# GNN layer on one core: gathered rows get 32 slots in three of four passes, with a ramp at each pass's start

## The reference, cut to what matters

```python
h = relu(layernorm(x))
h = _gcn_conv(h, src, dst, ones, W1, b1, n)          # pass 0: sum of h[src] per dst, 256 wide after W1
h = h / max(norm(h), 1e-12)
ev  = sigmoid(h[src] @ We1[:H] + h[dst] @ We1[H:])    # a gate for each edge
na  = relu(segment_sum(ev[:, None] * h[src], dst) @ Wn1 + bn1)     # pass 1
ev2 = sigmoid(na[src] @ We2[:H] + na[dst] @ We2[H:])
g   = relu(segment_sum(ev2[:, None] * na[src], dst) @ Wn1 + bn1)   # pass 2
out = _gcn_conv(g, src, dst, ev2, W2, b2, n)          # pass 3, weighted with ev2
return x + out
```

## Time and profile before

| what | value |
|---|---|
| time, median of 3 runs | 3329.52 us (3324.85 to 3332.83) |
| the profiled execution | 3348.71 us, its span 3346.9 us |
| granted TensorE clock, mean | 0.924 |
| busy shares | PE 79%, DVE 63%, ACT 48%, POOL 56% |
| gathers of pass 0 | 129.8 to 899.4 us |
| gathers of pass 1 | 1068.1 to 1701.8 us |
| gathers of pass 2 | 1841.2 to 2535.6 us |
| gathers of pass 3 | 2657.1 to 3288.3 us |
| dense steps of passes 1, 2, 3 end at | 1740.9, 2600, 3322.0 us |

### The profile page before, as it was taken

One profiled execution on the slowest core, in us unless ns is written; L12 is line 12 of the kernel. 1 busy time (PEld: TensorE's weight loads), 2 busy tenths in 40 slices (PEclk: granted clock), 3 DMA queues, 4 the chain that ended last, 5 costly groups with the idle time before them and its releaser, 6 DMA issues.

```text
span 3346.9 us, 58780 instructions
## 1 busy us (share of the span) xinstructions
PE 2635.7 (79%) x16470; PEld 2291.0 (68%) x16470; DVE 2111.6 (63%) x6199; ACT 1617.9 (48%) x3249; POOL 1866.2 (56%) x1816
## 2 busy tenths in 40 slices
PE   0667667898997677777789899999999676777775
PEld 0344446888885667666678788888888566666665
DVE  5567676665635566666675567666676456666667
ACT  7256565666666454554454444444444422233232
POOL 5345456555405666667720666666661267776673
PEclk9788898999999898988899899999999888888998
DMA  4244445555542333333322444444442433333333
GB/s 114 80 147 152 147 155 192 193 208 211 189 174 78 100 100 106 107 98 114 99 71 79 124 134 135 135 135 135 134 134 81 141 98 97 107 106 100 112 99 94
DMA packets 185594, 419.58 MB, mean 125 GB/s; under 512 B 36655, under 2 KB 136700, under 8 KB 175533
## 3 DMA queue, kind: packets, MB, share of 16 engines
q10 hardware_dynamic: 83703, 244.23, 20.6%
q0 software_dynamic: 61472, 140.49, 15.3%
q1 hardware_dynamic: 40118, 31.23, 3.0%
HBM read 311.35 MB, written 102.16 MB: 124 GB/s over the span
## 4 chain that ended last, share of the span: by engine, by line
PE 67%; issue 13%; DVE 9%; ACT 3%; ACTq 3%; another core or an unknown queue 2%; DMA 1%; DVEq 1%; POOL 1%; SPq 0%; POOLq 0%
PE ps L1117 18%; PE ps_high L1109 16%; PE ps_high L1117 12%; PE ps L1057 7%; PE ps_high L1075 3%; PE ps L1041 3%; ACT tab_area L769 2%; PE ps_high L1070 2%; ACTq L377 1%; PE ps_high L1196 1%; DVE acc L1592 1%; DVE tab_area L1521 1%; PE ps L1229 1%; DVE weights L1568 1%
## 5 line engine op out<-in xcount | busy, mean ns | idle before, releaser
L601 POOL DMA_INDIRECT rows<-table,edge_src x1664 | 1759.9, 1058 | 1164.0 <-SPq L496 604.0
L1109 PE MATMUL ps_high<-rows,weights 128*128 x2784 | 648.0, 342 | 385.2 <-issue 235.6
L1117 PE MATMUL ps<-tab_area,acc 128*128 128x129 f32 (+2 forms) x4410 | 824.2, 327 | 7.4 <-issue 6.1
L1109 PEld LDWEIGHTS ps_high<-rows,weights 128*128 128x128 f32 x2784 | 473.6, 204 | 486.9 <-issue 292.9
L1117 PEld LDWEIGHTS ps<-tab_area,acc 128*128 128x128 f32 x4410 | 698.6, 206 | 52.3 <-issue 7.2
L863 ACT ACTIVATE step<-xbuf,rows 128x128 f32 x928 | 358.0, 394 | 690.4 <-PE ps_high L1109 312.8
L1592 DVE TENSOR_TENSOR acc<-acc 128x640 f32<-128x640 f32 x735 | 604.9, 823 | 102.3 <-ACT acc L872 64.7
L1117 PE MATMUL ps_high<-tab_area,acc 128*128 128x129 f32 (+2 forms) x2940 | 588.3, 326 | 0.3 <-issue 0.3
L1575 DVE TENSOR_TENSOR acc<-acc,ps_high 128x129 f32 (+1 forms) x948 | 335.1, 354 | 384.9 <-PE ps_high L1109 187.8
L769 ACT ACTIVATE tab_area<-ps_high x816 | 404.4, 496 | 304.9 <-PE ps_high L1075 178.7
L1117 PEld LDWEIGHTS ps_high<-tab_area,acc 128*128 128x128 f32 x2940 | 478.0, 206 | 29.8 <-issue 1.2
(11 more groups left out here) (242 smaller groups left out, 2177.8 us busy)
## 6 DMA issues: line engine op xcount, KB each, us to landing
acc<-counts ACTq DMA_DIRECT2D x105, 1120.0 KB
counts<-tab_area ACTq DMA_DIRECT2D x51, 1568.0 KB
acc<-counts ACTq DMA_DIRECT2D x25, 1568.0 KB
rows<-table,edge_src POOLq DMA_INDIRECT x1664
table<-tab_area SPq DMA_DIRECT2D x6, 903.0 KB, 4.8
table<-acc SPq DMA_DIRECT2D x7, 448.0 KB, 4.2
table<-tab_area SPq DMA_DIRECT2D x6, 455.0 KB, 3.9
table<-tab_area SPq DMA_DIRECT2D x6, 448.0 KB, 3.0
```

The costliest lines, as they stand in the source:

```text
L601: nc.gpsimd.indirect_dma_start(rows[:, t % UNROLL, 0:row_floats[k]], None, tables[k], bass.IndirectOffsetOnAxis(ap=edge_src[:, t:t + 1], a ...
L1109: nc.tensor.matmul(ps[DENSE_BANKS + m % PAIR_BANKS][:, 0:WIDTH[k]], weights[:, m % W_RING, :], rows[:, bass.ds(known["slots"][m % UNROLL], ...
L1117: ins = nc.tensor.matmul(ps[j][:, 0:WIDTH[k]], gate_blocks[:, n % S_RING, j * PART:(j + 1) * PART], table[:, h, 0:WIDTH[k]], start=(h == 0 ...
```

## The change

The ring of row slots gets 32 slots in passes 0, 1 and 3 (rows of 128 and 130 words) and keeps 16 in pass 2 (rows of 258 words). `rows` becomes 32 x 130 words a partition (before 16 x 258), and each pass sees it with a stride of its own row width. There are 32 `landed` semaphores; `landed_count` works out what a tile's semaphore has counted to, over passes with different rings. To have semaphores for them, a few others are merged into one each (`flags_sent`, `tab_stored`, `pool_scaled`), with larger counts.

A gather's wait no longer stands at the ring's size: gather t may be `ahead` = min(ring, 8 + t // 4) tiles ahead. The first ten gathers of a pass are free (before 16); gather 16 waits for the relay's entry 10 (before 6), gather 24 for entry 16 (before 14); from gather 32 on the wait is the looser one, and from gather 96 on POOL may be 26 tiles ahead of the relay instead of 10. In pass 2 `ahead` ends at 16 with gather 32, which is the wait of before.

As slots differ between passes, DVE computes `pair_row`'s slot numbers anew for 16 slots after pass 1 and for 32 after pass 2 (`row_slots`).

```diff
+FIRST_AHEAD = 8
+SLOT_RING = 32
+ROW_RING = (SLOT_RING, SLOT_RING, UNROLL, SLOT_RING)
...
-        rows = sb("rows", [PART, UNROLL, ROW])
+        rows = sb("rows", [PART, SLOT_RING * ROW1])
...
+        rows_of = [within(rows, 0, [ROW_RING[k], row_floats[k]]) for k in range(4)]
...
-        landed = [sem(f"landed{u}") for u in range(UNROLL)]
+        landed = [sem(f"landed{u}") for u in range(SLOT_RING)]
...
+        def landed_count(k, t):
+
+            slot = t % ROW_RING[k]
+            earlier = sum(HALF // ROW_RING[q] for q in range(k) if slot < ROW_RING[q])
+            return 16 * (earlier + t // ROW_RING[k] + 1)
...
-                        sp.wait_ge(landed[u], tiles_before(k) + 16 * (i + 1))
+                        sp.wait_ge(landed[(i * UNROLL + u) % ROW_RING[k]], landed_count(k, i * UNROLL + u))
                         sp.sem_inc(tiles_landed[k], 1)
 
                         sp.wait_ge(pairs_done[k], entered[u])
...
-                pool.wait_ge(tab_stored[k], 16 * (NODE_TURNS if k == 0 else len(PIECES)))
+                pool.wait_ge(tab_stored, 16 * (NODE_TURNS + k * len(PIECES)))
                 for t in range(HALF):
-                    if t >= UNROLL:
-
-                        pool.wait_ge(slots_free, tiles_before(k) + t - UNROLL + LAG + 1)
-                    nc.gpsimd.indirect_dma_start(rows[:, t % UNROLL, 0:row_floats[k]], None, tables[k],
-                                                 bass.IndirectOffsetOnAxis(ap=edge_src[:, t:t + 1], axis=0)).then_inc(landed[t % UNROLL], 16)
+                    ahead = min(ROW_RING[k], FIRST_AHEAD + t // 4)
+                    if t >= ahead:
+
+                        pool.wait_ge(slots_free, tiles_before(k) + t - ahead + LAG + 1)
+                    nc.gpsimd.indirect_dma_start(rows_of[k][:, t % ROW_RING[k], :], None, tables[k],
+                                                 bass.IndirectOffsetOnAxis(ap=edge_src[:, t:t + 1], axis=0)).then_inc(landed[t % ROW_RING[k]], 16)
...
-                                         ACT.Sigmoid, bias=rows[:, bass.ds(slot, 1), SOURCES[k]])
+                                         ACT.Sigmoid, bias=rows_of[k][:, bass.ds(slot, 1), SOURCES[k]])
...
-                        known["slots"] = load_pairs(TEN, k, 1, m // UNROLL, UNROLL - 1)
+                        known["slots"] = load_pairs(TEN, k, 1, m // UNROLL, ROW_RING[k] - 1)
...
-            chain(single(pair_row[:, 1, :], pair_row[:, 2, :], 15.0, ALU.add))
-            chain(single(pair_row[:, 1, :], pair_row[:, 1, :], UNROLL - 1, ALU.bitwise_and))
+            def row_slots(ring):
+                chain(single(pair_row[:, 1, :], pair_row[:, 2, :], float(ring - 1), ALU.add))
+                chain(single(pair_row[:, 1, :], pair_row[:, 1, :], ring - 1, ALU.bitwise_and))
+
+            row_slots(SLOT_RING)
...
-            v.wait_ge(tab_stored[1], 16 * len(PIECES))
+
+            row_slots(UNROLL)
+            v.wait_ge(tab_stored, 16 * (NODE_TURNS + len(PIECES)))
             nc.vector.memset(tab3[:, :, ONE:ONE + 1], 1.0)
...
             nc.vector.tensor_single_scalar(stat[:, 0, :], acc3[:, 0:NODE_TILES, ONE], 1.0, ALU.add).then_inc(sqrt_need, 1)
+            row_slots(SLOT_RING)
             rooted(2)
             chain(nc.vector.reciprocal(dinv2[:, :], dinv2[:, :]))
```

More of the change, by code:

```diff
@@ L239, in gnn_kernel @@
         below = within(spare_sums, 2 * GROUP * PART, [2, GROUP, PART])
-        between = rows[:, :, :].rearrange("p a b -> p (a b)")
+        between = rows[:, :]
+        rows_of = [within(rows, 0, [ROW_RING[k], row_floats[k]]) for k in range(4)]
         staged = within(between, 0, [GROUP, HID])
@@ L321, in gnn_kernel @@
         centred, squared = sem("centred"), sem("squared")
-        tab_ready, tab_stored = [sem(f"tab_ready{k}") for k in range(2)], [sem(f"tab_stored{k}") for k in range(4)]
+        tab_ready, tab_stored = [sem(f"tab_ready{k}") for k in range(2)], sem("tab_stored")
         w1T_sent, w1T_ready, b1_rep_ready, w_prod, w_prod_ready = (
@@ L946, in _ @@
             pe.wait_ge(disorder_ready, 1)
-            nc.tensor.matmul(ps[5][0:1, 0:1], disorder, ones[:, 0:1], start=True, stop=True).then_inc(disorder_sent, 1)
+            nc.tensor.matmul(ps[5][0:1, 0:1], disorder, ones[:, 0:1], start=True, stop=True).then_inc(flags_sent, 1)
             pe.wait_ge(unsorted_ready, 1)
@@ L966, in _ @@
                 last = nc.tensor.matmul(ps[h][:, 0:TABLE // 2], ones[0:1, :], first[0][:, h * (TABLE // 2):(h + 1) * (TABLE // 2)], start=True, stop=True)
-            last.then_inc(first_sent, 1)
+            last.then_inc(flags_sent, 1)
             pe.wait_ge(half_ready, 1)
-            nc.tensor.matmul(ps[6][:, 0:1], ones[0:1, :], half_f[0:1, 1:2], start=True, stop=True).then_inc(low_sent, 1)
+            nc.tensor.matmul(ps[6][:, 0:1], ones[0:1, :], half_f[0:1, 1:2], start=True, stop=True).then_inc(flags_sent, 1)
             pe.wait_ge(ld_const, 64)
@@ L1041, in multiply @@
                     ins = nc.tensor.matmul(ps[m % FIRST_BANKS][:, 0:FEAT], weights[:, m % (2 * QUAD), :],
-                                           rows[:, bass.ds(first_pass.slots[u], 1), 0:FEAT].rearrange("p o f -> p (o f)"), start=True, stop=True)
+                                           rows_of[0][:, bass.ds(first_pass.slots[u], 1), 0:FEAT].rearrange("p o f -> p (o f)"), start=True, stop=True)
                     if m >= FIRST_BANKS:
```

28 lines of the change are left out of this document (14 added, 14 removed).

## The result

The changed kernel takes 3354.39 us (median of 4, 3352.25 to 3363.27) against 3331.18 us of before (median of 4): a ratio of 1.0085, 95% interval 1.0066 to 1.0103. It is slower by some 0.85%, on this chip.

The account below looks back on a forecast made before the run. It took pass 2 as PE-bound and passes 1 and 3 as paced by something tied to gathers. Terms summed to -17.5 us, about -15.5 after keeping 2: 3333 us profiled, 3314 us median, 8-in-10 range 3258 to 3345.

Parts of the forecast that it names:

- Term 1: End of passes 1 and 3: 16 more tiles done at the faster pace without gathers, -16 us together.
- Term 2: Start of passes 1 and 3: POOL stops about 6.2 us earlier, shortening PE's first long gaps, -6 us.
- Term 3: Three stretches of 61 gathers without a pause: consumers go faster if the extra lead is in stock, -8 us.
- Term 4: Tiles 32 to 96, ring filling: skipped POOL pauses lengthen three or four PE holds by 3.5 us each, +12 us.
- Term 5: DVE's added slot-number operations: hidden by a wait after pass 1, delaying the reciprocal after pass 2, +0.5 us.
- Pass 0 and pass 2 at nothing: Pass 0 waits for other things than tiles; pass 2 keeps ring 16 with PE 99% busy: 0 us each.
- rival "slower": Passes 1 and 3: completions arrive only once POOL pauses, so holds grow, 21 us a pass; 3370 us, chance 0.20.
- rival "nothing changes": Passes 1 and 3: gathers cost the same, free slots only shift PE's pauses, stock isn't lacking; 3330 us, chance 0.22.

Follow-up runs that it names:

- the ramp to 16: Kernel before with its 16 slots, 8 tiles ahead at first and one more each fourth gather up to 16, masked waits: 3326.99 us, ratio 1.0001, first kind.
- 32 at once: Changed kernel without its ramp, first 32 gathers of passes 0, 1 and 3 free, masked waits: 3384.49 us (1.0163) first kind, 3184.23 us (0.9992) second kind.
- 9 ahead: Kernel before with every gather at most 9 tiles ahead instead of 16, masked waits: 3417.19 us, ratio 1.0257, first kind.

## Why the prediction was wrong

It said 3314 us and faster; it is 3354 and slower. By its terms, of the traces of before and after, passes 1 and 3 together:

- *Term 1, the end, -16.* Right in mechanism and size: from step 200 on before takes 107.2 and 98.6 us, after 97.0 and 90.4, together -18.4 us (-14.3 against the ramp to 16).
- *Term 2, the start, -6.* Step 5 comes 6.5 and 6.4 us earlier, and PE's longest "issue" gaps of the first 55 us are 7.25 and 3.78 us where they were 9.16 and 13.00; in the ramp to 16 they are shorter too (7.26 and 4.55). But by step 15 only 1.3 and 1.8 us are left. The ramp only postpones the gathers whose price is paid at the start. Together -3, half of the size.
- *Term 3, the stretches short of supply, -8.* From step 50 to 200 before takes 409.3 and 410.1 us, after 403.5 and 408.0: -7.9 us. That this is the forecast size is partly luck: against the ramp to 16 (405.7 and 410.0) it is -4.2, and no run shows that the gain lies in the stretches that the term names.
- *Term 4, filling the ring, +12.* **This is the step that failed.** From step 15 to 50 before takes 96.6 and 97.3 us, after 118.7 and 119.2: +44 us. The prediction called it the dearest open term and took three or four holds of 3.5 us over both passes, each to grow from 3.08 to 6.60. The sign that it set for itself, PE gaps of 6 us and more between tiles 32 and 96, did not appear (5.87 is the longest). The runs show another rule for the size: each tile that is put in the ring costs the consumers of the first kind 1.3 to 1.4 us, about one gather's time on POOL, and there are 16 of them in each pass. "32 at once" pays the same 22 us in one piece at the start. The 3.5 us were misread from the rows: the place with 6.60 us was called one without a pause, but POOL pauses there for 2.70 us; and the gaps don't grow with the gathers before them in all four cases, as 22 gathers go with 6.60 and with 9.16 us and 19 with 13.00.
- *Term 5, DVE, +0.5.* 0.8 us after pass 2, nothing after pass 1.
- *Pass 0 and pass 2 at nothing.* Pass 2 is right. In pass 0 the relay's entry 10 is 7.7 us earlier in after and entry 150 7.5 later, so 15 us are paid there too. By entry 400 they are gone (889.1 us, 890.8 in before); PE is busy for 268.27 of the 300 us from 600 to 900 us in before, and it may be this half that takes them up. With 32 at once they are not taken up.

The terms inside the passes are -18 - 3 - 8 + 44 = +15 us as measured, where the prediction has -16 - 6 - 8 + 12 = -18; nearly the whole error is term 4. Passes 1 and 3 of the two traces differ by 4.8 + 9.8 = 14.6. Against the trace of the ramp to 16, nearer to its median, the difference is 14.5 + 11.3 = 25.8 us. The medians of before and after differ by 23 us.

The rival "slower" had the right sign and the right place: it priced the filling at 21 us a pass, and the runs have 22. That the price fits is in part luck. It was made of six holds a pass that grow from 3.08 to 6.60 us, and there are no such holds; PE's standing time grows by 11 us a pass, not 21. Its total of 3370 was 16 too high, since it gave terms 1 and 3 nothing, and they paid back 26.

Its reason, that completions reach the others only once POOL pauses, agrees in part. In pass 1 of before POOL pauses for over 1 us 51 times, 75.8 us in all, and in 47 of these pauses a rise of PE's is recorded that is over 0.5 us late. But of the 134 rises recorded that late while the gathers of pass 1 are made 87 lie outside such pauses, so "only" is wrong. And as POOL's pause ends with a release that itself needs a rise of PE's, the order of cause stays open; no run varied the pauses alone. What is shown is the size and the place of the loss, that it follows the tiles put in stock, and that it is absent where counts are on time.

What should have been a warning is that the ring was nearly full at most times, with POOL 8 or 9 tiles over the relay where 10 is the cap, and that the consumers hardly ever waited for a landing: a larger stock was not what they lacked, as the rival "nothing changes" says.

The rule of the Trainium skill by which PE never waits on anyone for its ports ("SBUF — State Buffer", section "SBUF: two separate sides") was no help here. It speaks of ports, and what came late were counts, PE's own to the others among them (0.96 us in pass 1). On the second kind of chip, where counts arrive in 0.014 us, the rival "nothing changes" holds (0.9984).

## What to carry to other kernels

Before deepening a ring, look who waits for whom: if the consumers wait for landings (156 us here on one kind of chip), the ring is empty, and its size made no difference from 12 slots to 32; if the producer waits for slots and the consumers for nothing, the ring is full, and more slots are only more work moved ahead of its need. It can be made too small all the same (9 ahead cost 89 us). Count the producer's operations and the consumers' steps in the same stretch of before and after: 79 gathers against 77, and 35 steps against 43, tell where the gain had gone. And ask what a producer that doesn't pause does to the others, because a buffer is free only if filling it is.

## What the runs showed of the hardware that was not expected

- Two kinds of chips: the same kernel takes 3328 us on two of the chips and 3185 on three others. The difference lies mostly in passes 1 and 3 (about 660 us against 593 and 606), where gathers run and PE isn't busy, and pass 2 is 751 against 740 us. On the slower one a rise of a count by PE is recorded with a median of 0.8 to 1.0 us behind the matmul while the gathers of passes 1 and 3 run, on the other after 0.014 us. Without gathers the slower one has 0.014 us too, and so it has in pass 2 with them. Why it is so was not found out.
- A load of 16 words into registers takes 1.0 to 1.1 us on ACT, SP, PE and DVE; the same load as half words at a stride of two takes 3.26 us on SP, and with such loads the whole kernel took 88 us more.
- In the first 55 us of passes 1 and 3 on the first kind POOL issued 38 to 40 gathers in before, in after and in "32 at once", whatever number of slots it had.
